# Sending x's first row tile and the first weights ahead of the edge analysis in a graph layer plus mixture-of-experts kernel

## The reference

```python
x = x + gnn(layernorm(x), stack([src, dst]), W, b)
x = x + ffn(layernorm(x)[None], router_w, router_b, w1, b1, w2, b2, ln_w, ln_b)[0]

def gnn(x, edge_index, W, b):            # self edges are added
    h = einsum('nd,od->no', x, W) + b
    deg = count of edges by row;  norm = deg**-0.5 at both ends
    return segment_sum(norm[:, None] * h[col], row)

def ffn(hidden, ...):                    # top 2 of 8 experts
    logits = flat @ router_w.T + router_b; weights = softmax(top 2)
    out = sum over experts of weight * (gelu(flat @ w1.T + b1) @ w2.T + b2)
    return layernorm(out + hidden) * ln_w + ln_b
```

## Time and profile before

| | |
|---|---|
| median of 3 runs | 623.88 us |
| the runs | 625.24, 621.68, 623.88 us |
| profiled execution, first to last instruction (span) | 619.0 us |
| PE busy in the span | 533.6 us (86%) |
| DVE busy in the span | 470.0 us (76%) |
| mean granted TensorE clock, as a share of 2.4 GHz | 0.951 |

### The profile page before, as it was taken

One profiled execution on the slowest core, in us unless ns is written; L12 is line 12 of the kernel. 1 busy time (PEld: TensorE's weight loads), 2 busy tenths in 40 slices (PEclk: granted clock), 3 DMA queues, 4 the chain that ended last, 5 costly groups with the idle time before them and its releaser, 6 DMA issues.

```text
span 619.0 us, 12317 instructions
## 1 busy us (share of the span) xinstructions
PE 533.6 (86%) x3660; PEld 298.1 (48%) x3661; DVE 470.0 (76%) x1295; ACT 242.4 (39%) x358; POOL 193.9 (31%) x199
## 2 busy tenths in 40 slices
PE   1688999899999999995779999999999999999100
PEld 1244554445444555554564655556565656564000
DVE  8879869997174889898858778695868685755397
ACT  5333444324280243435534344343444443401470
POOL 3013000000001165656544535344452543151240
PEclk9999999999899999998699999999999999999655
DMA  6894320333327243445486969798897889173978
GB/s 234 326 380 139 58 46 10 72 77 60 57 95 279 103 158 141 167 138 201 127 303 168 271 211 233 251 231 254 219 263 200 260 222 284 28 166 77 263 209 279
DMA packets 59565, 112.34 MB, mean 181 GB/s; under 512 B 33490, under 2 KB 33903, under 8 KB 59504
## 3 DMA queue, kind: packets, MB, share of 16 engines
q1 hardware_dynamic: 49424, 80.02, 37.7%
q0 software_dynamic: 8896, 27.38, 21.3%
q10 hardware_dynamic: 1184, 4.20, 2.0%
HBM read 71.75 MB, written 33.67 MB: 170 GB/s over the span
## 4 chain that ended last, share of the span: by engine, by line
PE 77%; DVE 14%; issue 3%; DMA 2%; ACT 2%; DVEq 1%; POOL 0%; ACTq 0%; POOLq 0%; SPq 0%
PE ps L1794 7%; PE ps L1795 7%; PE ps L1913 7%; PE ps L1914 6%; PE ps L1915 6%; PE ps L1892 5%; PE ps L1893 5%; PE ps L1894 5%; PE ps L1703 4%; PE ps L1642 4%; PE ps L1705 4%; PE ps L1704 4%; PE ps L1874 4%; DVE wbufs L1279 2%; PE ps L1623 2%
## 5 line engine op out<-in xcount | busy, mean ns | idle before, releaser
L613 POOL DMA_INDIRECT acc_rows<-work,ids_out x24 | 53.0, 2208 | 106.1 <-DVE work L1497 106.1
L1794 PE MATMUL ps<-wbufs,rows_and_counts 128*128 128x512 f16 x200 | 75.8, 379 | 0.5 <-DVE wbufs L1279 0.5
L1892 PE MATMUL ps<-rows_and_counts,wbufs 128*128 128x336 f16 (+2 forms) x256 | 74.9, 298 | 1.4 <-DVE rows_and_counts L1437 0.8
L1795 PE MATMUL ps<-wbufs,rows_and_counts 128*128 128x512 f16 x200 | 75.8, 379 | 0.0
L1893 PE MATMUL ps<-rows_and_counts,wbufs 128*128 128x336 f16 (+2 forms) x256 | 74.9, 298 | 1.0 <-issue 1.0
L1894 PE MATMUL ps<-rows_and_counts,wbufs 128*128 128x336 f16 (+2 forms) x256 | 74.9, 298 | 0.0
L1913 PE MATMUL ps<-wbufs,rows_and_counts 128*128 (+1 forms) x192 | 72.9, 379 | 1.6 <-issue 1.3
L1452 DVE SCALAR_TENSOR_TENSOR wbufs<-stage,wbufs 128x1024 f16<-128x1024 f32 x56 | 67.2, 1218 | 8.4 <-ACT wbufs L927 8.3
L1914 PE MATMUL ps<-wbufs,rows_and_counts 128*128 (+1 forms) x192 | 72.8, 379 | 0.0
L1915 PE MATMUL ps<-wbufs,rows_and_counts 128*128 (+1 forms) x192 | 72.8, 379 | 0.0
L526 POOL TENSOR_TENSOR work<-work 128x1024 f16<-128x1024 f32 x9 | 19.2, 2130 | 168.9 <-ACT work L900 168.9
(11 more groups left out here) (308 smaller groups left out, 1054.1 us busy)
## 6 DMA issues: line engine op xcount, KB each, us to landing
stage<-wst_in SPq DMA_DIRECT2D x72, 512.0 KB
acc_rows<-work SPq DMA_DIRECT2D x10, 512.0 KB
x_rows<-work SPq DMA_DIRECT2D x10, 512.0 KB
t<-x_in SPq DMA_DIRECT2D x1, 4096.0 KB, 14.0
wbufs<-b_in ACTq DMA_DIRECT2D x8, 512.0 KB
wbufs<-acc_rows SPq DMA_DIRECT2D x8, 512.0 KB, 6.2
t<-x_in SPq DMA_DIRECT2D x1, 3072.0 KB, 11.6
t<-x_in SPq DMA_DIRECT2D x1, 2048.0 KB, 7.8
```

What stands on the lines that cost most here:

```text
L1794: mm(o, ct_hi[:, cs], hs[:, at:at + HALF], start=(m == 0), stop=False, skip_group_check=True)
L1795: mm(o, ct_hi[:, cs], hs[:, D + at:D + at + HALF], start=False, stop=False, skip_group_check=True)
L1892: mm(o, wbufs[:, ds(w + ws, P)], x_hi, start=(j == 0), stop=False)
```

## The change

Six groups of instructions change places. None is added, none removed, and none changes its size.

- SP sends x's first row tile first, then weight pieces 0 to 3, and only then `dst_rows`, x's second row tile, the bias row, `src` and `dst`.
- ACT does `norm_std(0)` first, and `xt_hi(0)` before `weight_hi(3)`. Scaling the bias row comes after `weight_hi(3)`; the issue of the bias DMA comes after `xs_hi(1)`.
- DVE works row tile 0 and pieces 0 to 3 before the analysis of `dst_rows`; the reduction of the turned spans stands behind `weight_lo(7)`.
- PE starts with `turn(0)`. The four turns of the spans stand between `linear(0, 1)` and `linear(0, 2)`, the three sums behind `linear(0, 3)`.

```diff
@@ SP
+            sp.dma_start(t[:, 0:D], x[0:P, :]).then_inc(x0_in, 16)
+            for q in range(STAGES):
+                piece(q, False)
             sp.dma_start(dst_r[:, 0, :], dst_rows[0:P, :]).then_inc(dst_rows_in, 16)
             sp.dma_start(dst_r[0:ET - P, 1, :], dst_rows[P:ET, :]).then_inc(dst_rows_in, 16)
-            sp.dma_start(t[:, 0:D], x[0:P, :]).then_inc(x0_in, 16)
+            sp.dma_start(t[:, D:2 * D], x[P:2 * P, :]).then_inc(x1_in, 16)
             sp.dma_start(bias_row, b.partition_broadcast(1)).then_inc(b_in, 16)
             sp.dma_start(src_i[:], src).then_inc(edges_in, 16)
             sp.dma_start(dst_i[:], dst).then_inc(edges_in, 16)
-            for q in range(STAGES):
-                piece(q, False)
-            sp.dma_start(t[:, D:2 * D], x[P:2 * P, :]).then_inc(x1_in, 16)
@@ ACT
+            norm_std(0)
+            weight_hi(0)
+            weight_hi(1)
+            xs_hi(0)
+            weight_hi(2)
+            xt_hi(0)
+            weight_hi(3)
             act.wait_ge(b_in, 16)
             scaled_of.link(a.activation(bias_row, bias_row, ACT.Copy, scale=WSCALE))
             a.activation(bias2[0:1, :], bias_row, ACT.Copy).then_inc(bias_hi_done, 1)
-            weight_hi(0)
-            norm_std(0)
-            weight_hi(1)
-            xs_hi(0)
-            weight_hi(2)
-            weight_hi(3)
-            xt_hi(0)
             norm_std(1)
             weight_hi(4)
+            weight_hi(5)
+            xs_hi(1)
             act.wait_ge(bias_lo_done, 1)
             act.dma_start(bias2[1:2, :], bias_lo[0:1, :]).then_inc(bias_in, 16)
-            weight_hi(5)
-            xs_hi(1)
@@ DVE
+            dve.wait_ge(x0_in, 16)
+            norm_stats(0)
+            norm_rstd(0)
+            xn_of(0)
+            weight_lo(0)
+            xs_lo(0)
+            weight_lo(1)
+            weight_lo(2)
+            xt_lo(0)
+            weight_lo(3)
             dve.wait_ge(dst_rows_in, 32)
...
             v.engine_nop().then_inc(spans_cols, 1)
-            dve.wait_ge(x0_in, 16)
-            norm_stats(0)
-            dve.wait_ge(spans_tr, 1)
...
-            v.tensor_reduce(span[0:NW, 5:6], steps_in[0:NW, :], AXX, ALU.add).then_inc(spans_n, 1)
-            norm_rstd(0)
...
-            weight_lo(3)
             dve.wait_ge(x1_in, 16)
             norm_stats(1)
             weight_lo(4)
...
             weight_lo(7)
+            dve.wait_ge(spans_tr, 1)
...
+            v.tensor_reduce(span[0:NW, 5:6], steps_in[0:NW, :], AXX, ALU.add).then_inc(spans_n, 1)
             dve.wait_ge(edges_in, 32)
@@ PE
-            pe.wait_ge(consts_done, PE_CONSTS)
-            pe.wait_ge(spans_cols, 1)
...
             turn(0)
             linear(0, 0)
             linear(0, 1)
+            pe.wait_ge(consts_done, PE_CONSTS)
+            pe.wait_ge(spans_cols, 1)
...
+            ins.then_inc(spans_tr, 1)
             linear(0, 2)
             turn(1)
             linear(0, 3)
+            pe.wait_ge(spans_n, 1)
...
+               stop=True).then_inc(spans_ps, 1)
             pe.wait_ge(ranges_done, 1)
```

More of the change, by code:

```diff
@@ L1135, in _ @@
             v.engine_nop().then_inc(spans_cols, 1)
-            dve.wait_ge(x0_in, 16)
-            norm_stats(0)
+            dve.wait_ge(x1_in, 16)
+            norm_stats(1)
+            weight_lo(4)
+            norm_rstd(1)
+            xn_of(1)
+            weight_lo(5)
+            xs_lo(1)
+            weight_lo(6)
+            weight_lo(7)
             dve.wait_ge(spans_tr, 1)
@@ L1716, in _ @@
             linear(0, 1)
+            pe.wait_ge(consts_done, PE_CONSTS)
+            pe.wait_ge(spans_cols, 1)
+            for i, vv in enumerate((first_v, last_v)):
+                for h in range(2):
+                    ins = nc.tensor.transpose(misc_ps[:, (2 * i + h) * P:(2 * i + h + 1) * P], vv[:, h, :], ident[:])
+            ins.then_inc(spans_tr, 1)
             linear(0, 2)
@@ L1719, in _ @@
             linear(0, 3)
+            pe.wait_ge(spans_n, 1)
+            mm(misc_ps[0:1, 0:NW], span[0:NW, 5:6], tri[0:NW, :], start=True, stop=True)
+            mm(misc_ps[0:1, NW:2 * NW], span[0:NW, 5:6], ident[0:NW, 0:NW], start=True, stop=True)
+            mm(misc_ps[0:1, 2 * NW:3 * NW], span[0:NW, 3:4], ident[0:NW, 0:NW], start=True,
+               stop=True).then_inc(spans_ps, 1)
             pe.wait_ge(ranges_done, 1)
```

## The result

| | before | after |
|---|---|---|
| median of 6 runs | 624.56 us (621.68 to 626.11) | 629.4 us (628.32 to 632.15) |
| profiled execution, span | 619.0 us | 627.5 us (629.22 in all) |
| PE busy | 533.6 us | 538.5 us |

The forecast was 627.1, +3.2. Two executions further down, one of 843 us (e4) and one of 3134 us (p1), lie far off all others and stand in no ratio.

The account below looks back on a forecast made before the run. DVE was taken to bound the opening, PE the rest. A +3.5 us shift, less 1.57 absorbed, left +1.9; net +1.3 for the clock made +3.2: 627.1 us, range 623.7 to 630.3 (own range 625.8 to 628.5).

Parts of the forecast that it names:

- rivals 2 and 3: PE's clock falling sooner, from 22 to 30 us (629.8, chance 0.15); late landings of bias DMA or `dst_rows` (629.5, 0.05).
- T7: Moment DVE's list ends with the weights, 30.6 us before; forecast at 30.1, 0.5 us earlier.
- the copy: DVE's copy of PE's three sums, forecast to start at 35.95 us instead of 32.42.
- register loads: DVE's loads between the integers and `xt_lo(1)`, carried over at 2.33 us.
- from `linear(1, 0)` to `linear(2, 0)`: PE's stretch from 40.9 us to 58.5, including the loss to a cold clock.
- The start: First matmuls on PE: `linear(0, 0)` starts at 15.7 us instead of 19.19.
- DVE gives it back: DVE does the analysis at 16.65 to 19.7, taking 3.0 us, so T7 is only 0.5 us earlier.
- The sums behind `linear(0, 3)`: DVE must wait for PE's late sums; `ranges_done` and `xt_lo(1)` shift by +3.5 us (bounds +2.5 and +5).
- rival 2: PE's clock falls from 22 to 30 us, so `turn(1)` and 13 matmuls run cold: +2.7 more, 629.8, chance 0.15.
- The clock in the gap before `linear(1, 0)`: PE idles from 35.9 to 40.9, its clock falls near 39.5, and 2.2 us are lost, net +1.3.
- The old wait for tile 2: PE's old idle time ahead of `linear(2, 0)` absorbs 1.57 of the 3.5 us shift, leaving +1.9.
- The bias DMA: Issued at 25.5 instead of 21.93, it lands at 31.0 and adds 0.1 to 0.2 us on PE.

Follow-up runs that it names:

- e4: Changed kernel without POOL's subtraction for the bias row's low part, which is set to zero: 628.49 us, ratio 1.0070 to the kernel before.
- p1: Kernel before with only PE's three sums moved behind `linear(0, 3)`: 627.21 us, ratio 1.0051 to the kernel before.
- e1: Changed kernel with PE's three sums moved between `turn(1)` and `linear(0, 3)`: 624.11 us, ratio 1.0048 to the kernel before.
- e2: Changed kernel with 22 unread matmuls filling PE's waits from 23 to 30 us: 630.76 us, ratio 1.0158 to the kernel before.
- e5: Changed kernel with SP's nine sends of zero rows moved behind the transposing DMA of tile 2: 628.78 us, ratio 1.0059 to the kernel before.
- a0: The changed kernel run once more, with no edit: 627.57 us, ratio 1.0115 to the kernel before.
- p2: Changed kernel with SP's old order of sends for x and the first pieces: 631.62 us, ratio 1.0138 to the kernel before.
- c1: Changed kernel with sums ahead of `linear(0, 3)`, no POOL bias subtraction, and zero-row sends behind tile 2's transpose: 623.95 us, ratio 0.9997 to before.
- e3: Changed kernel with 22 unread matmuls in PE's early waits and 28 more behind the sums: 625.54 us, ratio 1.0072 to the kernel before.
- b1: Kernel before with SP's nine zero-row sends moved behind the transposing DMA of tile 2: 622.11 us, ratio 0.9950 to the kernel before.
- b3: Kernel before with zero-row sends behind tile 2's transpose, DVE's integers ahead of `weight_lo(4)`, register loads spread out: 618.65 us, ratio 0.9893 to before.
- b2: Kernel before with DVE's integers ahead of `weight_lo(4)` and register loads spread out, sends unmoved: 625.71 us, ratio 1.0031 to the kernel before.

## Why the forecast was right in kind and short in size

The measured 629.4 lies inside the stated range, but 2.3 us above the forecast and outside its own range of 625.8 to 628.5; the nearest numbers are those of rivals 2 and 3 (629.8 and 629.5). The way from the earlier trace rows's 55.32 to 62.74, in the terms of the forecast:

| term | forecast | after | shown by |
|---|---|---|---|
| T7 against 30.6 | -0.5 | +0.8 | e4 |
| from T7 to the copy, before 1.8 | 5.85 | 7.5 | e1, p1, e2 |
| so the copy | +3.5 | +6.5 | |
| register loads, before 2.33 | 2.33 | 4.09 (+1.8) | e5 |
| from `linear(1, 0)` to `linear(2, 0)`, before 17.9 | 17.6 (-0.3) | 17.05 (-0.9) | trace |
| `linear(2, 0)` | +3.2 | +7.4 | |

1. *The start: right.* x's tile lands 3.5 us after its issue, at 4.4 as taken. `linear(0, 0)` starts at 15.69, forecast 15.7. That is 3.5 of the 5.4 us of analysis moved, two thirds and not the nine tenths that the forecast says; nothing else was worked out from that share.
2. *DVE gives it back: right in kind, T7 mis-sized by 1.3 us.* I let the analysis take 3.0 us and took the one stall of before out of it, since POOL would not be filling a row then. But the change moves ACT's `bias_hi` too, and with it POOL's subtraction of 2.11 us, which now runs beside the analysis. I had asked who waits for POOL, not what its running does to DVE. The landing of pieces, for which my bounds were made, was not the cause. The Trainium skill states this contention, in "SBUF — State Buffer", section "Who interferes with whom": DVE's `tensor_scalar` in a two-port mode and a GpSimd operation exclude each other for the whole instruction, while a DVE instruction with one SBUF input outside these modes and `tensor_reduce` do not meet it. The rows agree: the pair waits, and the statistics beside POOL's subtraction in before took their usual 1.28 us. In which mode the pair ran, no row shows.
3. *The sums behind `linear(0, 3)`: right, and the main cause.* DVE waits 3.86 us for PE. With the clock up (e2) copy and T7 are 5.7 us apart, with 5.85 forecast. Alone in the kernel before (p1) the copy came at 36.09, forecast 35.95 (5.5 us behind T7, with 5.85 forecast), and the kernel lost 3.2 us, as forecast for the whole.
4. *Which rival happened: rival 2, beside the forecast.* I held it at 0.15, with 2.7 us. The clock fell at 25.6, in the first burst behind a gap, and 7.2 us passed from T7 to the end of `linear(0, 3)` instead of 5.1. From T7 to the copy this is 1.8 us more than with the clock up (7.5 and 5.7), in a0 1.4. The 2.7 was mis-added: its own two terms, 0.76 for the turn and 13 x 0.21 for the matmuls, make 3.5, so that it came near the number is luck. It was no rival of the forecast but a term of it: the clock fell in this stretch in after, a0, e1, e4, e5, p2 and c1, and not in e2 and e3 with the gaps filled. The Trainium skill's rule on idle gaps between bursts ("TensorE: Matmul & The Clock Gate", "Why this matters for your kernels"), which I used for the gap at 36, speaks of longer gaps than these of at most 2.2 us; here it differs from the rows, and the rows decide.
5. *Register loads: a step that I left out.* I carried 2.33 us over without asking what they would stand beside 6 us later. 1.8 us (e5).
6. *The clock in the gap before `linear(1, 0)`: right.* It fell (0.76 over 40 to 45), and stayed down until 49.5; from 45.69 that costs some 1.9 us.
7. *The old wait for tile 2 absorbs 1.57 us: right.* PE has no wait ahead of `linear(2, 0)`. Landing of the transposing DMAs after, as forecast:

```profile
DMA to landing us min/median/max: 4.3/4.3/4.7
```

8. *The bias DMA: right.* It is issued at 26.8, 1.3 late as all of T7's part, takes 5.4 us to land, and the bias matmul does not start later for it (its weight load waited 0.8 us, but it follows the matmul ahead of it by 0.57 us, as it does in b1 by 0.56); where PE came there with the clock up (e2), it waited 0.19 us, with 0.1 to 0.2 forecast.

The terms missed (1.3 at T7, 1.7 up to the copy, 1.8 in the loads) less 0.6 that was better than forecast make the 4.2 between +3.2 and +7.4. The median moved by 4.8 us only. From `linear(2, 0)` to the end after needs 564.8 us and before 563.7; after has one more fall of the clock, at 325 to 330 (0.66, or 1.7 us). The rest of the difference between 8.5 and 4.8 lies in the execution of before that was profiled: its 619.0 and the 1.7 us around the span make 620.7, 3.9 below the median of 624.56. The traces of b1 and b3, whose later parts are the same, show falls near 110 and near 320 that it does not have, 1.7 us each. That before's other executions have those falls is likely, since two of them are 3.4 us. The mean granted clock of each execution points the same way: on the chip of p1 it was 0.952 and 0.951 in before's executions of 620.0 and 620.6 us, 0.943 and 0.944 in those of 628.25 and 628.13 (but 0.945 in one of 620.75). Only one execution of before was traced, so where the falls lie stays open. I had taken the whole 4.9 between span and median to lie around the span; all but 1.7 of it was that one traced execution being a fast one. The terms came out 4.2 us short against that trace, and only 1.6 short against the median of 624.56: the number was nearer than the working deserved, and that part is luck.

## What to carry to other kernels

Work that is moved off the front of a queue is put behind something else: ask first who reads its result, and where in the other engine's list it now stands; here three tiny matmuls behind `linear(0, 3)` cost 3.2 us by themselves (p1), and the whole change some 5. Of each moved instruction ask also what runs beside it at the new time on the other engines and in the transfers, as its old duration holds only for its old neighbours. An earlier first matmul is worth nothing as long as the stretch behind it is bound by another engine; the gain was to be had the other way round (b3), by reading the small result early and freeing the transfer that was late next.

## What the runs showed of the hardware

- *Register loads were slower beside sends from SBUF to DRAM.* Three loads on DVE's queue took 2.33 us in before and without the nine sends (e5, b1; c1 2.34), 3.04 to 3.37 in p1, e4 and p2, and 3.92 to 4.19 in after, a0 and e1 to e3. The rate alone does not do it: 404 GB/s were moved beside the 2.33 us of before, and 412 beside the 4.09 of after.
- *A small POOL operation holds up DVE.* POOL's subtraction on one partition, 1024 elements in 2.11 us, stretched two DVE operations of 128x40 from 0.38 to 1.65 us, while in before two statistics beside it kept their 1.28 us.
- *Short gaps can be enough for the clock.* In after PE had run at 2.4 GHz up to 23.0, waited 2.18 us, and fell in the next burst, at 25.6 (0.56 in 25 to 30). In a0 it fell behind waits of 0.89 and 2.00 us, in c1 behind 0.66 and in the 2.00 us that followed; filling the waits kept it at 1.00. It is not sure to fall: with waits of 0.2 to 0.6, 1.5 and 0.3 us it stayed up in before and p1 and fell at 29.7 in b1 (0.69 in 30 to 35), where the work up to there is the same.
- *The clock's falls are not the same in each execution.* One costs 1.7 us or a multiple, as (1 - clock) x 5 over its stretches of 5 us shows. It comes or stays away at 105 to 125 and at 315 to 330, and costs 1.7 or 3.4 at 160 to 180, in kernels with the same work there; after and a0, the same kernel, differ so. Before's own runs on one chip spread over 7 to 8 us (617.1 to 624.2, 620.2 to 627.1, 620.0 to 628.3). Terms below 2 us were therefore read from marks in the traces.
- *A transfer behind a backlog landed when the backlog let it.* The first transposing DMA took 9.4 us when asked for sooner (b2) and 7.8 in before, landing at 55.3 and 55.2, and at most 4.8 once the nine sends stood behind it (b1, b3).
